# A selective-scan stage: every TensorE product padded to 128 rows and 128 columns, and the decay matrix rectified and exponentiated on ScalarE one block ahead

## What is computed

```python
zxbcdt = u @ W_in + b_in                      # u: layer-normed input, 256 channels
z  = zxbcdt[..., :512]
xs = zxbcdt[..., 512:1024]                    # 8 heads of 64
Bm = zxbcdt[..., 1024:1088]                   # STATE = 64
Cm = zxbcdt[..., 1088:1152]
dt = softplus(zxbcdt[..., 1152:] + dt_bias)   # one per head
decay = exp(dt * -exp(A_log))
# for each token t:  h = decay_t * h + (dt_t * xs_t) outer B_t ;  y_t = h . C_t
y = (y + D_skip * xs) * silu(z)
out = y @ W_out + b_out
```

## Time and profile before

| what | us |
|---|---|
| median of three runs (range) | 2029.82 (2028.94 to 2030.76) |
| the profiled execution | 2031.91 |
| its span, first to last instruction | 2030.1 |
| PE busy in the span | 1773.4 (87%) |
| DVE busy | 1278.0 (63%) |
| ACT busy | 613.3 (30%) |
| POOL busy | 547.0 (27%) |
| the scan's loop, from its second to its last job | about 1036 to 1400 in the span |

### The profile page before, as it was taken

How to read it: one execution, slowest core, us unless ns; L and a number is a source line. 1 busy time by engine, 2 the same in 40 slices (tenths; PEclk the granted TensorE clock), 3 DMA queues, 4 the chain that set the end, 5 groups by cost and what they waited for, 6 DMA issues and landing times. The chain is left out here.

```text
span 2030.1 us, 25408 instructions
## 1 busy us (share of the span) xinstructions
PE 1773.4 (87%) x9053; PEld 1385.7 (68%) x9053; DVE 1278.0 (63%) x2605; ACT 613.3 (30%) x992; POOL 547.0 (27%) x415
## 2 busy tenths in 40 slices
PE   6889989859999899799579999997889885999996
PEld 4678878748857788577347667665745544888885
DVE  6775675554444466347568778776678963566553
ACT  2223333333314244241322232331110022444442
POOL 2111120000000023114434344343300002466663
PEclk9899999969999899899789999998589997999998
DMA  5000000100100001110321111111110004565552
GB/s 192 1 1 1 1 1 1 45 0 1 42 0 1 11 11 34 34 58 16 125 85 51 46 43 53 44 43 53 62 38 21 21 21 137 137 146 124 151 123 32
DMA packets 72350, 101.81 MB, mean 50 GB/s; under 512 B 14271, under 2 KB 53323, under 8 KB 72013
## 3 DMA queue, kind: packets, MB, share of 16 engines
q1 hardware_dynamic: 58316, 82.23, 12.2%
q0 software_dynamic: 12288, 17.31, 4.8%
q10 hardware_dynamic: 1664, 1.18, 0.2%
HBM read 76.61 MB, written 23.47 MB: 49 GB/s over the span
## 5 line engine op out<-in xcount | busy, mean ns | idle before, releaser
L2437 POOL DMA_INDIRECT out<-k_eo,idx x64 | 120.6, 1885 | 117.1 <-DVE k_eo L2508 102.5
L1288 PE MATMUL d_pO<-d_xn,mod 128*128 128x256 f32 x512 | 121.5, 386 | 2.9 <-ACT mod L1168 2.9
L1333 PE MATMUL d_pO<-d_sp,d_raw 128*128 128x257 f32 x512 | 116.1, 385 | 2.6 <-ACT d_raw L1182 2.6
L1333 PEld LDWEIGHTS d_pO<-d_sp,d_raw 128*128 128x128 f32 x512 | 97.0, 192 | 17.5 <-ACT d_raw L1182 3.5
L1288 PEld LDWEIGHTS d_pO<-d_xn,mod 128*128 128x128 f32 x512 | 94.6, 192 | 17.1 <-ACT mod L1168 6.0
L61 PE MATMUL b_pO<-b_vh,b_ph 128*128 128x256 f32 x302 | 89.0, 295 | 12.7 <-DVE b_pl L601 12.7
L1718 ACT ACTIVATE g_dlm<-g_dlm 128x1024 f32<-128x1024 f32 x32 | 33.9, 1060 | 197.8 <-DVE g_dlm L1771 197.8
L2469 ACT ACTIVATE k_act_g<-k_pg 128x512 f32<-128x512 f32 x64 | 38.3, 598 | 163.4 <-PE k_pu L63 160.8
L496 ACT ACTIVATE b_p<-b_pS,b_nmax 128x2048 f32<-128x2048 f32 (+14 forms) x32 | 40.6, 1269 | 154.9 <-DVE b_nmax L617 154.9
L63 PE MATMUL b_pO<-b_vl,b_ph 128*128 128x256 f32 x302 | 86.6, 287 | 0.0
L62 PE MATMUL b_pO<-b_vh,b_pl 128*128 128x256 f32 x302 | 86.6, 287 | 0.0
(11 more groups left out here) (416 smaller groups left out, 5228.7 us busy)
## 6 DMA issues: line engine op xcount, KB each, us to landing
g_cumb<-cum_dram SPq DMA_DIRECT2D x32, 512.0 KB, 3.7
k_wf<-in_WgT SPq DMA_DIRECT2D x16, 512.0 KB
k_wf<-in_WuT SPq DMA_DIRECT2D x16, 512.0 KB
k_wf<-in_WdT SPq DMA_DIRECT2D x16, 512.0 KB
rows_dram<-h_hx SPq DMA_DIRECT2D x8, 544.0 KB, 3.0
x<-in_x SPq DMA_DIRECT2D x8, 512.0 KB, 10.0
d_w<-in_w SPq DMA_DIRECT2D x4, 1024.0 KB, 6.2
uT_dram<-d_ug SPq DMA_DIRECT2D x16, 256.0 KB, 2.4
```

What stands on the lines that cost most here:

```text
L1288: last = nc.tensor.matmul(pO[:, et % 2, 0:C], eT[g % 2][:, j * P:(j + 1) * P], xn[:, g * GT + j, :], start=g == 0 and j == 0, stop=g == NG ...
L1333: last = nc.tensor.matmul(pO[:, t % 2, 0:PW], raw[:, e, t * P:(t + 1) * P], proc[:, e, :], start=e == 0, stop=e == E - 1)
L2437: nc.gpsimd.indirect_dma_start(out=out, out_offset=bass.IndirectOffsetOnAxis(ap=column(e, t), axis=0), in_=eo[:, e % 2, t, :], in_offset=None,
```

## The change

All of it lies in `decays` and `state_space`.

- **Padding.** The bias operands get 128 rows instead of 2 (`bb`, `onesr`; rows beyond the second are zero in `bb`). `bc` keeps B and C in two slots of 128 columns, of which 64 are filled and 64 are zeroed once; so the transposes of `state_rows` and `pst` have 128 columns, and `bcT` and `H` have 128 rows, of which 64 are zero. Every matmul of the scan then has 128 active rows and 128 active columns. The zeroing is one more memset on DVE ahead of the scan.
- **Decay.** The eight DVE instructions and the slot `dd` are gone. ACT computes `relu(cum_s - cum_t)` for each head, with the per-token sum as a bias operand read from memory, into a slot of `le` that there now is for each batch, and then `exp(-x)` over all heads in place. It does so for job n+1 in the step of job n, between `by_state(n+1)` and `high(n+2)`; for job 0 it does so ahead of the first copies. SP's loads wait for the new semaphore `dd_done` in place of `lcm_done`.

```diff
@@ decays
-        b2, bh = sb("f_b2", [2, DT0]), sb("f_bh", [2, DT0], FR)
+        b2, bh = sb("f_b2", [P, DT0]), sb("f_bh", [P, DT0], FR)
-            sp.dma_start(b2[:], w["b_in"][0:DT0].partition_broadcast(2)).then_inc(s["b_in"], 16)
+            sp.dma_start(b2[:], w["b_in"][0:DT0].partition_broadcast(P)).then_inc(s["b_in"], 16)
-            nc.scalar.copy(m.ones2[:], m.ones[0:2, :])
+            nc.scalar.copy(m.onesr[:], m.ones[:])
@@ state_space
-        bc = sb("g_bc", [P, B, 2 * STATE])
-        bcT = sb("g_bcT", [STATE, B, 2, P])
+        bc = sb("g_bc", [P, B, 2, P])
+        bcT = sb("g_bcT", [P, B, 2, P])
-        dd, le, mt = [m.dlm[:, k] for k in range(3)]
-        H = sb("g_H", [STATE, B, INNER])
+        le, mt = m.dlm[:, 0:B], m.dlm[:, B]
+        H = sb("g_H", [P, B, INNER])
@@ sync
-                    sp.wait_ge(s["lcm_done"], (n - 1) * HEADS)
+                    sp.wait_ge(s["dd_done"], (n - 1) * HEADS)
@@ scalar
-                nc.scalar.copy(bc[:, b], pbc[:, 0:2 * STATE]).then_inc(s["bc_copied"], 1)
+                nc.scalar.copy(bc[:, b, :, 0:STATE], pbc[:, 0:2 * STATE].rearrange("p (k n) -> p k n", k=2)).then_inc(s["bc_copied"], 1)
+            def decay(job):
+                i, b = job
+                n = num(job)
+                act.wait_ge(cs_in[b], (i + 1) * 48)
+                act.wait_ge(s["m_done"], least(n - 1))
+                for h in range(HEADS):
+                    nc.scalar.activation(le[:, b, h, :], cumb[:, b, h, :], ACT.Relu, bias=cs[:, b, 3, h:h + 1],
+                                         scale=-1.0).then_inc(s["dd_done"], 1)
+                act.wait_ge(s["dd_done"], (n + 1) * HEADS)
+                nc.scalar.activation(le[:, b], le[:, b], ACT.Exp, scale=-1.0).then_inc(s["le_done"], 1)
             high((0, 0))
             high((0, 1))
+            decay((0, 0))
+            act.wait_ge(s["zeroed"], 1)
             evacuate((0, 0))
...
-                if cur:
-                    n = num(cur)
-                    act.wait_ge(s["lcm_done"], (n + 1) * HEADS)
-                    act.wait_ge(s["m_done"], n)
-                    nc.scalar.activation(le, dd, ACT.Exp).then_inc(s["le_done"], 1)
                 if nxt:
                     evacuate(nxt)
...
                 if nxt:
                     by_state(nxt)
+                if nxt:
+                    decay(nxt)
                 if nxt and after(nxt):
                     high(after(nxt))
@@ vector
+            nc.vector.memset(bc[:], 0.0).then_inc(s["zeroed"], 1)
             nc.vector.memset(H[:], 0.0)
...
-                for h in range(HEADS):
-                    nc.vector.tensor_scalar(dd[:, h, :], cumb[:, b, h, :], cs[:, b, 3, h:h + 1], 0.0,
-                                            ALU.subtract, ALU.min).then_inc(s["lcm_done"], 1)
@@ tensor
-                    last = nc.tensor.matmul(dst[:, 0:width], ones2[:], bb[:, o:o + width], start=False, stop=True)
+                    last = nc.tensor.matmul(dst[:, 0:width], onesr[:], bb[:, o:o + width], start=False, stop=True)
-                    last = nc.tensor.transpose(pbt[0:STATE, k * P:(k + 1) * P], bc[:, b, k * STATE:(k + 1) * STATE], m.ident[:])
+                    last = nc.tensor.transpose(pbt[:, k * P:(k + 1) * P], bc[:, b, k, :], m.ident[:])
-                    nc.tensor.matmul(pst[0:STATE, :], bc[:, b, 0:STATE], xw[:, b], start=True, stop=True).then_inc(s["st_ready"], 1)
+                    nc.tensor.matmul(pst[:], bc[:, b, 0, :], xw[:, b], start=True, stop=True).then_inc(s["st_ready"], 1)
```

More of the change, by code:

```diff
@@ L1546, in _ @@
             dve.wait_ge(s["b1"], 1)
-            nc.vector.tensor_scalar(bh[:], bh[:].bitcast(F32), m.ident[0:2, 0:1], None, ALU.mult).then_inc(s["b2"], 1)
+            nc.vector.tensor_scalar(bh[:], bh[:].bitcast(F32), m.ident[:, 0:1], None, ALU.mult).then_inc(s["b2"], 1)
             dve.wait_ge(s["b2"], 1)
-            nc.vector.scalar_tensor_tensor(out=m.bb[:], in0=b2[:], scalar=m.ident[0:2, 1:2], in1=bh[:].bitcast(F32), op0=ALU.mult, op1=ALU.add)
+            nc.vector.scalar_tensor_tensor(out=m.bb[:], in0=b2[:], scalar=m.ident[:, 1:2], in1=bh[:].bitcast(F32), op0=ALU.mult, op1=ALU.add)
             dve.wait_ge(s["wogh"], 1)
@@ L1581, in state_space @@
         sb, ps, sem = setup(nc, ctx)
-        winh, winl, wogh, wogl, bb, ones2, cumb = m.winh, m.winl, m.wogh, m.wogl, m.bb, m.ones2, m.cumb
+        winh, winl, wogh, wogl, bb, onesr, cumb = m.winh, m.winl, m.wogh, m.wogl, m.bb, m.onesr, m.cumb
         dskip = sb("g_dskip", [P, HEADS])
@@ L1598, in state_space @@
         names = ("loaded ip_ready bc_copied xs_copied th_done bt_ready bt_copied g_ready gm_done "
-                 "zr_done lcm_done le_done m_done dtx_done xw_done xD_done i_ready st_ready y_ready "
+                 "zr_done zeroed dd_done le_done m_done dtx_done xw_done xD_done i_ready st_ready y_ready "
                  "t1_done t2_done y_done hs_done h_done yg_done yT_ready yh_done yl_done o_ready x_done uh_done ul_done").split()
@@ L1784, in body @@
                 dve.wait_ge(s["y_ready"], n)
-                nc.vector.tensor_tensor(mt, le, over(gm[:, b], HEADS), ALU.mult).then_inc(s["m_done"], 1)
+                nc.vector.tensor_tensor(mt, le[:, b], over(gm[:, b], HEADS), ALU.mult).then_inc(s["m_done"], 1)
                 dve.wait_ge(s["i_ready"], n + 1)
@@ L1788, in body @@
                 dve.wait_ge(s["h_done"], n)
-                nc.vector.tensor_tensor(heads(H[:, b]), heads(H[:, b]), wide(et[:, b], STATE), ALU.mult).then_inc(s["hs_done"], 1)
+                nc.vector.tensor_tensor(heads(H[0:STATE, b]), heads(H[0:STATE, b]), wide(et[:, b], STATE), ALU.mult).then_inc(s["hs_done"], 1)
                 if prev:
@@ L1793, in body @@
                 dve.wait_ge(s["st_ready"], n + 1)
-                nc.vector.tensor_tensor(H[:, b], H[:, b], pst[0:STATE, :], ALU.add).then_inc(s["h_done"], 1)
+                nc.vector.tensor_tensor(H[0:STATE, b], H[0:STATE, b], pst[0:STATE, :], ALU.add).then_inc(s["h_done"], 1)
                 if nxt:
@@ L1819, in step @@
                 if cur:
-                    decay(cur)
                     body(cur, prev, nxt)
@@ L2622, in program @@
             m.wogh, m.wogl = sb("g_wogh", [P, B, INNER // P, C], FR), sb("g_wogl", [P, B, INNER // P, C], FR)
-            m.bb, m.ones2 = sb("g_bb", [2, DT0], FR), sb("g_ones2", [2, P], FR)
+            m.bb, m.onesr = sb("g_bb", [P, DT0], FR), sb("g_onesr", [P, P], FR)
             m.dlm, m.cumb = sb("g_dlm", [P, 3, HEADS, P]), sb("g_cumb", [P, B, HEADS, P])
```

2 lines of the change are left out of this document (1 added, 1 removed).

## The result

The changed kernel takes 2051.8 us in the median, against 2029.68 for the kernel before on the same chip: a ratio of 1.0104, 95% interval 1.0076 to 1.0133. It is about 1% slower. The forecast was 2012.3 with a range of 1998 to 2030, so the sign was wrong and the time lies outside the range. The profiled execution took 2055.59 us.

What follows compares the result with a forecast made beforehand. PE was taken as the bound at 11.67 us per job, then the loop through ACT at 11.13. Gains of 15.7 (29 periods) and 2.8 (end), less 0.6 and 0.4 (start), took 2029.82 to 2012.3 us, range 1998 to 2030.

Steps and rivals of the forecast that it cites:

- What bounds the kernel now: In the scan, PE sets the pace, busy 358.33 of 360 us at 11.67 us per job; only shortening its sequence helps.
- Part 1, the padding: On PE, full-size matmuls avoid gaps at size changes: sequence 9.81 us instead of 11.67, gaining 1.86 per job.
- Part 2, the closed loop: From project through state_rows, by_state, Relus, exponential, high and low to the next project: 11.13 us per job, setting the pace.
- The Relus: On ACT between by_state and the exponential: spacing 0.27 us, length 0.39, eight 2.28; memory operand 0.12 of spacing each.
- The hops: Starts on another engine after by_state's transposes, high and low: 0.04 us each.
- The 1.3 us of PE's time per job that turn idle ahead of project: PE waits for low before project; the first matmul after the wait gives way 0.33 us instead of 0.23 later.
- Start and end: Outside the 29 periods: 0.6 and 0.4 us lost at the start, 2.8 gained at the end.
- rival 1: PE keeps the pace at 9.81 us, the eight Relus fitting into 0.96: 1973 us, chance 0.04.
- rival 2: The Relus' memory operand is free: loop 10.19 us, total 1984, chance 0.08.
- rival 3: Padding gives nothing back, PE's gaps having another cause than active array size: loop 12.62 us, 2059, slower, chance 0.06.
- rival 4: The Relus cost what L1191 does: loop 12.00 us, total 2038, slower, chance 0.06.
- rival 5: No change: Relus at 0.34 us spacing and a further hop or two put the loop at 11.6 to 11.7, chance 0.07.

Runs made afterwards that it cites:

- experiment 1: The changed kernel with high moved ahead of the next job's decay on ACT: 1979.0 us, ratio 0.9758.
- experiment 2: The kernel before with the padding alone, the decay staying on DVE and the exponential at the head of ACT's step: 1989.03 us, ratio 0.9804.
- experiment 9: The changed kernel with the Relus' memory operand, the subtraction of the token's own sum, left out: 2002.57 us, ratio 0.9874.
- experiment 5: The kernel of experiment 1 with the bias matmuls put back to two rows: 2009.61 us, ratio 0.9909.
- experiment 6: The kernel of experiment 1 with the state side put back to 64 rows or columns, bias still padded: 1993.09 us, ratio 0.9827.
- experiment 4: The changed kernel with eleven filler matmuls of unread results ahead of each project from job 2 on: 2025.36 us, ratio 0.9986.
- experiment 7: The changed kernel with five filler matmuls of unread results ahead of each project from job 2 on: 2026.67 us, ratio 0.9987.
- experiment 3: The kernel before with the decay's move to ACT alone, products left narrow: 2129.83 us, ratio 1.0497.
- experiment 10: The kernel of experiment 4 with PE waiting for low last of four and DVE for high after its other wait: 2023.62 us, ratio 0.9973.

## Why the prediction was wrong, step by step

- **What bounds the kernel now:** right. PE set the pace at 11.67, and what shortens PE's sequence shortens the kernel when nothing else gets in the way (experiments 1 and 2).
- **Part 1, the padding:** right in every term that the trace shows. In the undisturbed job shown px to pz is 1300.93 - 1299.25 = 1.68 us and pz to the transposes 1.63, against 2.02 and 2.03 before and a forecast of 1.63 for both. state_rows starts 6.31 us into the step, forecast 6.29. The whole sequence, forecast 9.81, runs at 9.84 to 9.86 in experiment 1.
- **Part 2, the closed loop:** right in its links and in their order. by_state starts 6.73 into the job (forecast 6.71), the Relus at 6.99 (6.97).
- **The Relus:** mis-sized by 0.17. The term was 2.28 us for eight, they take 2.45: the spacing is 0.29 and not 0.27, the length 0.39 as forecast. Two errors in it partly cancel. Without the operand, eight take 1.70 (experiment 9) where the prediction's lower bound had 1.34, a spacing of 0.20 and not 0.15; and the operand adds 0.094 to each, not the 0.12 of spacing that half of L1191's price had given. The estimate from the Trainium skill ("ScalarE: Activation LUTs", What ACT_TABLE_LOAD costs) was 2.45 for the eight, and the trace agrees; the skill's 93 ns per operand agrees with the 0.094 too. The Trainium skill also advises VectorE for relu, min and add, and does not name subtract ("ScalarE: Activation LUTs", Rules for kernel authors). This case bears that out where the Relus stand ahead of high (22 us slower than before, against 39 faster with the subtraction on VectorE, experiment 2), and not where they stand behind it (49 faster, experiment 1).
- **The hops,** the times from the end of an instruction to the start of the one on another engine that waits for it: mis-sized by 0.3 for the three together. Each was put at 0.04, from by_state's start behind the transposes in the one job of the earlier trace rows. In the job shown, low starts 0.16 after high ends, and project 0.24 after low ends; in the jobs in between it is 0.23 and 0.05. By_state's own hop is 0.04 and 0.15 in turn, and it was so in the kernel before: a second job would have shown it. Together with the Relus that is the undisturbed 11.57 instead of 11.13, 13 us.
- **The 1.3 us of PE's time per job that turn idle ahead of project:** the idle time was there (1.48), and this is the step that failed. It was priced at 0.10, the slower start after a wait. What it cost was the granted clock: in 18 of 29 jobs it was at 1.2 GHz for a part of project, and each of those jobs took 1.57 us more. The clock of 1.00 in the earlier trace rows was read as a given of this stretch, when it was the clock of an engine that was busy 358.33 of 360 us; the change took just that away. No rival had such a fall. Without the falls the larger loop alone would have given some 2025 us, inside the range; the falls took the result out of it.
- **Start and end:** +0.97 for +1.0 and -2.4 for -2.8, the first by luck. Job 1 came 0.9 earlier than forecast, since the padding helps there too, and the period behind it grew by 0.9 more than forecast, with a wait of 2.63 us and a slow clock. At the end the scan gained 1.8; the other 0.6 lie in later stages, where kernels with the same code there differ by more than that.
- **The rivals:** 1 is out as a forecast, though its pace exists (experiment 1). 2 is out by experiment 9: the operand is not free. 3 named the right sign for a reason that experiments 5 and 6 refute. 4 is out: the spacing is 0.29, not 0.38. 5, the loop at 11.6 to 11.7 by a further hop or two, is what an undisturbed job does (11.57), and without the falls the kernel would have been some 3 us below before (experiments 4 and 7), at the edge of what can be told from no change.

The net of it: the padding's 1.86 us per job was all there, and it was given up because one line in ACT's queue put 3.5 us of work, due only a job later, ahead of 0.4 us of work that PE needs next.

What stays open: why the clock falls in 18 jobs and not in the other 11, with waits of nearly the same length ahead of both, and why with narrow products it came back so much later (experiment 3). The runs show only that waits of up to 0.9 us, recurring in every job, left it at 1.00, and that waits of 1.1 to 1.5 did not. A single wait's length does not decide it either: ahead of project(2) a wait of 0.93 or 0.95 was followed by a fall (experiments 1 and 2), and waits of 1.33 and 2.04 behind filler matmuls were not (experiments 4 and 7).

## What to carry to other kernels

When an edit turns TensorE from the bound into an engine that waits for about a microsecond in every job, do not price the idle time at nothing: write down a rival in which the granted clock falls, and take its cost from matmuls at the lower level. When work is moved to an engine with time to spare, look at what stands behind it in that engine's queue and who waits for it; put what is due soonest first. Padding small products to the full array, where they stand between full ones, was worth 1.8 us of an 11.7 us job here, even though it adds arithmetic.

## What the runs showed of the hardware that I had not expected

- A wait of 1.48 us in a period of 11.6 us was enough for the granted clock to fall in most periods; 0.74 us in 10.8 and 0.89 us in 11.6 were not. Filler matmuls with unread results bought about 25 us (61 with narrow products).
- With narrow products most falls lasted far longer: 24 us at 0.50 with PE busy throughout (experiment 3), against less than 3.6 us in the job shown with full-size ones. One fall of experiment 3, at 1122 us, was as short.
- The order of waits ahead of an instruction can have a price of its own: with the last signal waited for first, PE started 0.244 us after it in every second job and 0.055 in the others; with it waited for last, 0.055 in all (experiment 10).
- Three bias matmuls of two rows cost 1.1 us per job merely by standing between full-size ones (experiment 5).
